# Reordering the last query pair and the context sums around a windowed cross attention

## What is computed

```python
x = x + _L0_xattn_ref(_layernorm(x), ctx_2048, itok, W_kvc, W_dq, W_uq, W_qr, W_uk, W_kr, W_uv, W_o)
# in it: 16 heads of 128, latent 128, rope 64
kv_c = kv @ W_kvc;  q_c = q @ W_dq
q_nope = q_c @ W_uq;  q_rope = _rope(q_c @ W_qr);  k_rope = _rope(kv_c @ W_kr)
scores = (q_nope . (kv_c @ W_uk) + q_rope . k_rope) * scale
good = (k_ids <= seg) & (k_ids >= seg - 8)           # 9 keys for each token
attn = softmax(where(good, scores, NEG))             # no good key: the mean over all keys
x = x + (attn . (kv_c @ W_uv)) @ W_o
...
x = x + _L1_xattn_ref(_layernorm(x), ctx_2048, ...)  # needs, for each batch, a decay-weighted sum and the mean of the context's 1601 rows
```

## Time and profile before

| | us |
|---|---|
| three runs | 1257.52, 1250.88, 1230.74 |
| median | 1250.88 |
| the profiled execution, own time | 1244.93 |
| its span | 1242.4 |
| TensorE matmuls busy | 1018.6 (82%) |
| VectorE busy | 720.4 (58%) |
| ScalarE busy | 494.1 (40%) |
| GpSimd busy | 266.7 (21%) |
| mean granted TensorE clock | 0.833 |

### The profile page before, as it was taken

One profiled execution on the slowest core, in us unless ns is written; L12 is line 12 of the kernel. 1 busy time (PEld: TensorE's weight loads), 2 busy tenths in 40 slices (PEclk: granted clock), 3 DMA queues, 4 the chain that ended last, 5 costly groups with the idle time before them and its releaser, 6 DMA issues.

```text
span 1242.4 us, 14589 instructions
## 1 busy us (share of the span) xinstructions
PE 1018.6 (82%) x5429; PEld 779.3 (63%) x5429; DVE 720.4 (58%) x1072; ACT 494.1 (40%) x755; POOL 266.7 (21%) x242
## 2 busy tenths in 40 slices
PE   6888898999989577777768896999734884899996
PEld 5775455667778466565667784435424873688885
DVE  6443672334466368897797853779977445333333
ACT  2453652112256354666576433334221421333331
POOL 2232330000035322033023200345403000022220
PEclk9997996558769788888888997999765565999998
DMA  8512355323011332223313103241030001111110
GB/s 286 204 55 68 123 179 198 106 72 140 22 57 66 103 126 95 101 86 116 106 51 116 38 18 106 98 139 81 18 137 0 1 1 54 35 60 58 51 34 34
DMA packets 51111, 106.87 MB, mean 86 GB/s; under 512 B 6564, under 2 KB 26844, under 8 KB 45934
## 3 DMA queue, kind: packets, MB, share of 16 engines
q1 hardware_dynamic: 50158, 95.48, 22.6%
q0 software_dynamic: 896, 10.62, 2.2%
HBM read 100.84 MB, written 5.24 MB: 85 GB/s over the span
## 4 chain that ended last, share of the span: by engine, by line
PE 57%; DVE 20%; ACT 10%; issue 4%; DMA 4%; POOL 2%; SPq 2%; POOLq 0%; ACTq 0%; DVEq 0%
PE banks L41 8%; PE banks L43 7%; PE banks L42 7%; PE banks L1944 4%; PE banks L1174 3%; DMA w_raw<-in_L_attn_Wk 2%; PE banks L1173 2%; PE banks L345 2%; PE banks L2256 2%; DVE tw_sum L1734 2%; PE banks L1206 2%; POOL w_low L1875 1%; PE banks L1956 1%; PE banks L2223 1%; ACT wa_cTh L751 1%
## 5 line engine op out<-in xcount | busy, mean ns | idle before, releaser
L156 POOL TENSOR_TENSOR w_low<-w_raw,w_high 128x1024 fp32r<-128x1024 f32 (+2 forms) x64 | 123.3, 1936 | 494.9 <-ACT w_high L152 494.8
L152 ACT CAST w_high<-w_raw 128x1024 fp32r<-128x1024 f32 (+3 forms) x66 | 53.7, 831 | 89.5 <-PE banks L43 45.7
L41 PE MATMUL banks<-da_xT_high,w_high 128*128 128x512 f32 x128 | 57.1, 446 | 26.9 <-ACT da_q L1359 21.2
L42 PE MATMUL banks<-da_xT_low,w_high 128*128 128x512 f32 x128 | 55.2, 431 | 0.0
L43 PE MATMUL banks<-da_xT_high,w_low 128*128 128x512 f32 x128 | 54.4, 425 | 0.0
L2344 POOL TENSOR_TENSOR hf_hl<-hf_h,hf_hh 128x512 fp32r<-128x512 f32 x16 | 20.6, 1291 | 155.1 <-ACT hf_hh L2398 155.1
L41 PE MATMUL banks<-hf_xhh,w_high 128*128 128x512 f32 x128 | 51.6, 403 | 0.0
L43 PE MATMUL banks<-hf_xhh,w_low 128*128 128x512 f32 x128 | 50.5, 394 | 0.0
L42 PE MATMUL banks<-hf_xhl,w_high 128*128 128x512 f32 x128 | 50.1, 391 | 0.0
L41 PEld LDWEIGHTS banks<-da_xT_high,w_high 128*128 128x128 f32 x128 | 27.1, 212 | 35.4 <-issue 29.6
L1944 PE MATMUL banks<-ff_xT_high,tw_guT 128*128 128x512 f16 x128 | 48.5, 379 | 0.0
(11 more groups left out here) (415 smaller groups left out, 2908.6 us busy)
## 6 DMA issues: line engine op xcount, KB each, us to landing
cs_rows<-in_ctx SPq DMA_DIRECT2D x24, 1024.0 KB, 5.1
tw_raw<-in_L_ffn_w_gate_up SPq DMA_DIRECT2D x32, 256.0 KB, 3.7
w_raw<-in_L_xattn_W_o SPq DMA_DIRECT2D x8, 512.0 KB
w_raw<-in_L_attn_Wq SPq DMA_DIRECT2D x8, 512.0 KB
w_raw<-in_L_attn_Wk SPq DMA_DIRECT2D x8, 512.0 KB
w_raw<-in_L_attn_Wv SPq DMA_DIRECT2D x8, 512.0 KB
w_raw<-in_L_attn_Wo SPq DMA_DIRECT2D x8, 512.0 KB
tw_raw<-in_L_ffn_w_proj SPq DMA_DIRECT2D x16, 256.0 KB, 3.8
```

The source lines that it names most:

```text
L41: nc.tensor.matmul(out, a[0], b[0], start=start, stop=False)
L42: nc.tensor.matmul(out, a[0], b[1], start=False, stop=False)
L152: self.nc.scalar.copy(self.wh[k][:, 0:cols], self.raw[k][:, 0:cols]).then_inc(self.split_hi[k], 1)
L156: self.nc.gpsimd.tensor_tensor(self.wl[k][:, 0:cols], self.raw[k][:, 0:cols], self.wh[k][:, 0:cols].bitcast(F32), ALU.subtract).then_inc(s ...
```

## The change

In the last pair, TensorE makes the rotary product ahead of the nope product, VectorE rotates ahead of its subtraction for qn, and ScalarE's copies of the rotated queries stand ahead of its qa copy. Of batch 2's sum one chunk stays ahead of the first scores; two chunks and the tail stand behind the scores of round 0, together with the means of batches 0 and 1. Two chunks of batch 3 stand in round 1. All later chunks and tails stand between the second and the third group of scores of their round (`sums(r)`), a round later than before; turns and means move with them by one round, and so do the waits and copies on ScalarE and VectorE.

```diff
@@ -789,10 +789,10 @@
                 high(1, i + 1)
             if i in (3, 6):
                 self.cs.scalar_sum(act, i // 3 - 1, 6)
+            if i == PAIRS - 1:
+                rotated(i)
             act.wait_ge(self.qa_done, 2 * i + 1)
             nc.scalar.copy(self.qa[:, :, i * 2], c.bank[:, 4, :]).then_inc(self.qa_out, 1)
-        rotated(PAIRS - 1)
-        self.cs.scalar_sum(act, 2, 3)
 
         act.wait_ge(self.qa_done, 2 * PAIRS)
         R = self.G // 4
@@ -810,11 +810,11 @@
                 nc.scalar.copy(self.cn[r % 3][:, :, :], c.bank[0:self.KEYS, 2, :].rearrange("p (g q) -> p g q", g=4)).then_inc(self.cn_out, 1)
                 act.wait_ge(self.s_sub, r + 1)
                 nc.scalar.activation(self.s[r % 3][:, :, :], self.s[r % 3][:, :, :], ACT.Exp).then_inc(self.e_done, 1)
-            if r % 3 == 1 and r < 14:
-                self.cs.scalar_sum(act, 3 + r // 3, 3)
+            if r == 0 or r % 3 == 2 and r < R:
+                self.cs.scalar_sum(act, 2 + (r + 1) // 3, 3)
             if r in (12, 13):
                 c.split_high(act, *self.slot_v(r - 12, 0), 2 * HD)
-            if r == R:
+            if r == R + 1:
                 c.split_high(act, *self.slot_y(0, 0))
 
         def high_out(i, k):
@@ -932,12 +932,16 @@
                 dve.wait_ge(self.kc_out, u)
             v.tensor_copy(self.kst[:, :, :], c.bank[:, 0, 0:3 * P].rearrange("p (j t) -> p j t", j=3)).then_inc(self.kst_out, 1)
 
+        def query_low(i):
+            for h in range(2):
+                dve.wait_ge(self.qn_hi, 2 * i + h + 1)
+                v.tensor_tensor(self.qn[1][h][:, :], c.bank[:, h, :], self.qn[0][h][:, :].bitcast(F32), ALU.subtract).then_inc(self.qn_lo, 1)
+
         for i in range(PAIRS):
             dve.wait_ge(c.split_hi[2], f[2] + 2 + i)
             v.tensor_tensor(c.wl[2][:, 0:2 * LAT], c.bank[:, 3, 0:2 * LAT], c.wh[2][:, 0:2 * LAT].bitcast(F32), ALU.subtract).then_inc(c.split_lo[2], 1)
-            for h in range(2):
-                dve.wait_ge(self.qn_hi, 2 * i + h + 1)
-                v.tensor_tensor(self.qn[1][h][:, :], c.bank[:, h, :], self.qn[0][h][:, :].bitcast(F32), ALU.subtract).then_inc(self.qn_lo, 1)
+            if i < PAIRS - 1:
+                query_low(i)
             dve.wait_ge(self.qr_done, i + 1)
             if i:
                 dve.wait_ge(self.qr_sum, 4 * i)
@@ -975,14 +981,14 @@
                 ch(v.tensor_reduce(mx[:, 0, :], s[:, :, :], AX.X, ALU.max))
                 ch.wait()
                 v.tensor_tensor(s[:, :, :], s[:, :, :], mx[:, 0, :].unsqueeze(2).broadcast_to([P, 4, self.KEYS]), ALU.subtract).then_inc(self.s_sub, 1)
-            if r == 0 or r % 3 == 2 and r < R:
-                self.cs.vector_mean(dve, 2 + (r + 1) // 3, 5)
-            if r == 1:
+            if r == 1 or r % 3 == 0 and r:
+                self.cs.vector_mean(dve, 2 + r // 3, 5)
+            if r == 0:
                 dve.wait_ge(self.cm_done, 1)
-                v.tensor_copy(self.cm[:, 0:3], c.bank[:, 5, 16:19]).then_inc(self.cm_out, 3)
-            if r % 3 == 0 and r:
+                v.tensor_copy(self.cm[:, 0:2], c.bank[:, 5, 16:18]).then_inc(self.cm_out, 2)
+            if r == 2 or r % 3 == 1 and r > 1:
                 b = 2 + r // 3
-                dve.wait_ge(self.cm_done, b - 1)
+                dve.wait_ge(self.cm_done, b)
                 v.tensor_copy(self.cm[:, b:b + 1], c.bank[:, 5, 16:17]).then_inc(self.cm_out, 1)
             if 1 <= r <= R:
                 s, mx, g4 = self.s[(r - 1) % 3], self.mx[(r - 1) % 3], slice(4 * r - 4, 4 * r)
@@ -998,7 +1004,7 @@
 
                 dve.wait_ge(self.o_done, r - 1)
                 t0, b = 32 * (r - 2), (r - 2) // 2
-                dve.wait_ge(self.cm_out, max(b + 1, 3))
+                dve.wait_ge(self.cm_out, max(b + 1, 2))
                 v.scalar_tensor_tensor(self.qa[:, t0:t0 + 32, :], self.inv[:, t0:t0 + 32].unsqueeze(2).broadcast_to([P, 32, H]), self.cm[:, b:b + 1],
                                        c.bank[:, 6 + r % 2, :].rearrange("p (t h) -> p t h", h=H), ALU.mult, ALU.add).then_inc(self.o_out, 1)
 
@@ -1106,7 +1112,8 @@
             ins.then_inc(self.uk_done, 1)
             if i == 0:
                 rope_turn(8)
-            for k, w_, done in ((0, 2 * HD, self.qn_done), (1, 2 * ROPE, self.qr_done)):
+            parts = ((0, 2 * HD, self.qn_done), (1, 2 * ROPE, self.qr_done))
+            for k, w_, done in parts if i < PAIRS - 1 else parts[::-1]:
                 pe.wait_ge(c.split_lo[k], f[k] + (k == 0) + 1 + i)
                 for h in range(2 - k):
                     out = c.bank[:, 2 if k else h, :]
@@ -1138,9 +1145,7 @@
                 cols = slice(h * LAT, (h + 1) * LAT)
                 mm3(nc, c.bank[:, 4 + h, :], (c.wh[2][:, cols], c.wl[2][:, cols]), (self.qn[0][h][:, :], self.qn[1][h][:, :]), True, True).then_inc(self.qa_done, 1)
 
-        for k in range(3):
-            self.cs.tensor_chunk(pe, 2, k, 3)
-        self.cs.tensor_tail(pe, 2, 3)
+        self.cs.tensor_chunk(pe, 2, 0, 3)
 
         R = self.G // 4
         pe.wait_ge(self.qa_out, 2 * PAIRS)
@@ -1151,6 +1156,14 @@
             for j in range(C):
                 ins = nc.tensor.matmul(c.bank[:, 5, 16:16 + n], self.wkvc[:, j, :], self.cs.meanT[:, j, b:b + n], start=(j == 0), stop=(j == C - 1))
             ins.then_inc(self.cm_done, 1)
+
+        def sums(r):
+
+            if 2 <= r < R - 1:
+                self.cs.tensor_chunk(pe, 3 + r // 3, r % 3, 3)
+                if r % 3 == 2:
+                    self.cs.tensor_tail(pe, 3 + (r - 2) // 3, 3)
+
         keys = lambda t: t.rearrange("p j t -> p (j t)")
         queries = lambda t, at: t[:, at:at + 8, :].rearrange("p t h -> p (t h)")
         for r in range(R + 2):
@@ -1172,6 +1185,8 @@
                     out = c.bank[:, n, q * K8:(q + 1) * K8]
                     nc.tensor.matmul(out, queries(self.qa, 8 * g), keys(self.kvcT[:, m, g % 16, :, :]), start=True, stop=False)
                     ins = nc.tensor.matmul(out, queries(self.qr[rows], 8 * (g % 32)), keys(self.krT[rows, m % 2, g % 16, :, :]), start=False, stop=True)
+                    if q == 1:
+                        sums(r)
                 ins.then_inc(self.s_done, 1)
                 if r >= 1:
                     pe.wait_ge(self.cn_out, r)
@@ -1179,23 +1194,19 @@
                     g = 4 * r + q
                     ins = nc.tensor.transpose(c.bank[0:K8, 2, q * P:(q + 1) * P], keys(self.kvcT[:, g // 16, g % 16, :, :]), c.ident[:, :])
                 ins.then_inc(self.cn_done, 1)
-            if r == 0 or r % 3 == 2 and r < R:
-                b = 2 + (r + 1) // 3
-                if b >= 3:
-                    pe.wait_ge(self.cm_out, b)
+            if r == 0:
+                means(0, 2)
+                self.cs.tensor_chunk(pe, 2, 1, 3)
+                self.cs.tensor_chunk(pe, 2, 2, 3)
+                self.cs.tensor_tail(pe, 2, 3)
+            if r == 1 or r % 3 == 0 and r:
+                b = 2 + r // 3
+                pe.wait_ge(self.cm_out, b)
                 self.cs.tensor_turn(pe, b, 5)
-            if r == 0:
+            if r == 1:
                 self.cs.tensor_chunk(pe, 3, 0, 3)
                 self.cs.tensor_chunk(pe, 3, 1, 3)
-            if r == 1:
-                self.cs.tensor_chunk(pe, 3, 2, 3)
-            if 2 <= r < 14:
-                self.cs.tensor_chunk(pe, 4 + (r - 2) // 3, (r - 2) % 3, 3)
-            if r % 3 == 1 and r < 14:
-                self.cs.tensor_tail(pe, 3 + r // 3, 3)
-            if r == 1:
-                means(0, 3)
-            if r % 3 == 0 and r:
+            if r == 2 or r % 3 == 1 and r > 1:
                 means(2 + r // 3, 1)
             if r >= 2:
                 pe.wait_ge(self.pt_out, r - 1)
```

## The result

| | before | after |
|---|---|---|
| median of 4 runs each, us | 1249.54 (1230.74 to 1257.52) | 1273.43 (1271.43 to 1278.63) |
| profiled execution, own time | 1244.93 | 1272.37 |
| its span | 1242.4 | 1270.6 |
| TensorE busy | 1018.6 (82%) | 1040.9 (82%) |
| VectorE, ScalarE, GpSimd busy | 720.4, 494.1, 266.7 | 722.3, 494.0, 266.6 |

What follows compares the result with a forecast made beforehand. The prediction took the stretch of scores to be bound by TensorE at its low clock. It summed the profiled 1244.9 us + 4.5 (rotation) + 0 (first rounds) + 19.6 (later rounds) to 1269 us, range 1237 to 1286.

Steps and rivals of the forecast that it cites:

- What bounds the stretch: Scores, between last query pair and value projection: bound by TensorE and its clock, only 44.0 us at 2.4 GHz after 203.5.
- Step 1: Last pair, rotating first: the queues of ScalarE and VectorE make the first scores start later, +4.5 us.
- Step 2: Context sums moved behind the first scores: exposed chunks against a removed 1.58 us wait, 0 us, ends -6.5 and +6.0.
- Step 3: Later chunks among the scores, 13 rounds: new waits for VectorE and less time at the high clock, +19.6 us.
- h: Share of the 13 rounds run at 2.4 GHz: 0.35 before, taken as 0.20 after, giving 144.0 us.
- rival B: The clock never rises in the rounds: +35 us there, +6.0 in the first rounds, 1290 us in total; chance 0.14.
- The wait for VectorE in every fast round: Before the transpose of probabilities at 2.4 GHz, TensorE waits 0.8 to 1.7 us, since the chunk no longer covers VectorE.
- Step 4: Behind the rounds: last mean and W_o's first load come a round later, 0 us, ends 0 and +2.
- A: The clock stays high because spread chunks even out TensorE's work in the rounds: 1223 us, faster; chance 0.09.
- C: The rounds keep their 0.35 share of high clock; only the waits and the later start count: 1259 us; chance 0.22.
- D: The change has no grip: chunks beside the scores cost nothing, the wait is as before; 1247 us; chance 0.12.

Runs made afterwards that it cites:

- the combined version: Changed kernel with the rotation edits undone, later chunks and tails back behind the transposes of keys, turn and means ahead of them: 1231.49 us, ratio 0.9952.

## Why the prediction was right

The forecast was 1269 us in a range of 1237 to 1286, same or slower. The median is 1273.43, and 1276.05 on a second chip. The forecast gave "same" 0.58 and "slower", by its line at 2%, 0.33; the interval of the ratio spans that line, so which of the two it was isn't settled. Point by point:

**What bounds the stretch** held: TensorE and its clock. Over the 40 runs of the kernel before, 1223 us went with a mean granted clock of 0.849 and 1262 us with 0.817, which is some 12 us for each 0.01. The changed kernel lies past the low end, at 0.813.

**Step 1, +4.5 us**, was right in size and mechanism: +4.9. Each link is in the timeline above: ScalarE's copies of pair 6 behind those of qn, the wait of TensorE (6 us expected, 6.56 found), the qa copy without cover. The run with ScalarE's order mended shows the cause by removing it. What I didn't foresee is how it adds up. In the ratios the step is worth nothing within the change (without it: 1.0328; with it: 1.0280 and 1.0329), but 2% on the kernel before. The traces show it within the change too: from the last pair's transposes of W_uk to the end of scores 15 the changed kernel took 199.1 and 196.7 us, 191.9 without the rotation edits and 189.7 with ScalarE's order mended. The clock ahead of the last pair hides these 5 to 9 us in the totals. On the kernel before, the late start came with slower rounds besides (132.0 us for 124.4); why is open.

**Step 2, 0 us**, was right: -0.5 us, with the wait ahead of the first transpose gone. It came as the middle of two ends (-6.5 and +6.0), with short rises at 197.5 and 207.8 us behind the two pairs of chunks. That it was the middle was luck: these rounds took 18.1 us in the run without the rotation and 17.1 with ScalarE's order mended, with 1.00 from 200.0 and from 198.8 us on, so near the lower end. The first group of scores, 1.6 us shorter, ran at 1.00: the clock was 0.51 over the long wait (177.0 to 182.8 us), 0.50 over the last qa products, and rose at 187.3 us, just ahead of these scores, where in the kernel before it fell at 189.9 us, early in them.

**Step 3, +19.6 us**, had the mechanism right and the size wrong: +30.4. The mis-sized term is "I take h = 0.20". From the end of scores 2 (212.4) to the fall at 214.6 us there are 2.2 us at 1.00, so h = 2.2 / 154.8 = 0.014. That is the rounds of rival B, whose bound of 159 us I had for them. It was too high by 4, most of it because I gave a chunk (1.86) to all 13 rounds where the last has none, and 1.80 us to means that took 1.50 in the round shown. B's term for the first rounds (+6.0) was wrong, and so its total of 1290. The second profiled execution of the changed kernel had 2.0 + 3.4 + 3.4 us at 1.00, h = 0.06. The row that should have set h was the one of 44.3 us at 0.50 with TensorE never idle: it showed the low clock in whole rounds that did have the chunk in their block, so a thinner block had little claim to any share.

**The wait for VectorE in every fast round** can hardly be judged. One fast round was left, and it had the wait, 1.00 us at 215.71. In the slow rounds only the one with the tail waits, 0.58 us each of four times (0.34 forecast). VectorE is no bound here.

**Step 4, 0 us**: +1.6 with the drain, at the lower clock.

**The total was nearer than its terms.** The profiled execution after began its last pair 6.6 us earlier, by luck of the clock upstream; without that it would have been 1279. The medians differ by 24 us, which is what the forecast had (1269 for 1244.9), since the median of before lies 4.6 us over its profiled execution. By the ratio the loss is some 35 us, and from the last pair on it's 34.8 us in the profiled executions: the 11 us beyond the forecast are those that step 3 was short of.

**Rivals.** A (1223) fell: in the changed order the clock didn't hold. Its rule in the Trainium skill, page "TensorE: Matmul & The Clock Gate", section "Why this matters for your kernels", is that continuous work releases the full clock. The trace disagrees: 158.06 busy of 161.00 us and no rise in this stretch of the run with only step 3. C (a share of 0.35 kept) and D (no grip) fell with the rounds. B was right on the rounds alone.

What is shown is that putting the chunks among the scores sends the rounds to 0.50 (the run with step 3 alone) and that their old place brings rises back. What stays open is why. That an unbroken block brings the rise is a reading: in the kernel before, three of the four blocks of transposes, chunk, tail and output products went with a rise (278.7, 302.6, 326.5 us), the first, from 238.66 to 245.21 us, had none, and rises also came within a turn, within means and among scores. No run varied one piece of the block's size in steps. Nor did any run settle what ends a stretch at 1.00: in the combined version the fall at 278.0 us came within scores, with no idle time at all ahead of it.

## What to carry to other kernels

Where TensorE has no idle time and yet the low clock, look at the order of its list: try to put the dense products (wide moving side) of a loop's turn into one unbroken piece, and to move the thin ones, with one or two columns or a part of the rows, to its far side. All of it together gave 1.5% here (0.9846); no single move was clear of the noise. Spreading the chunks among the scores is the opposite, and cost 3%, clear of the noise. And before one engine's list is reordered for an earlier start, follow the same data through the lists of the others: here ScalarE's order gave the gain away, and mending it only came out even.

## What wasn't expected of the hardware

TensorE ran at 1.2 GHz for 174 us while busy for 96% of them, and useless work put into 13 rounds gave three stretches of 10.2 us at 2.4 GHz and a fourth rise, and the kernel didn't measurably slow down (1.0247 for 1.0280 and 1.0329). Nearly the same instructions in another order gave 6.74 us for a round where the changed kernel takes 12. And the kernel before has no one time: the same code ran in 1223 to 1262 us, in step with its mean granted clock, so a change of 1% in such a stretch asks for ten runs of each and the clock beside them.
